# Attention values projected once in channel layout, with their taps on ScalarE and VectorE

## The chip, the cores and the metric

One core of a Trainium2 chip runs the whole program. The metric is the time of one execution on the device in microseconds. TensorE, VectorE, ScalarE, GpSimd and SyncE (the queue SP that starts DMAs) each have their own in-order instruction stream and hand work over through semaphores.

## The reference

Sixteen sequences of 750 tokens with 128 channels go through one layer: a token pooler that halves the length to 375, an attention block with 8 heads of 64, and a mixture of 16 experts with a shared path. Only the attention's projections matter here. `xn` is the normalized sequence, padded with two zeros ahead in time:

```
def _proj(xp, w1, wd):
    y = jnp.einsum('ed,bdn->ben', w1, xp)
    y = wd[None, :, 0:1] * y[..., :-2] + wd[None, :, 1:2] * y[..., 1:-1] + wd[None, :, 2:3] * y[..., 2:]
    return y
xp = jnp.pad(xn.transpose(0, 2, 1), ((0, 0), (0, 0), (2, 0)))
q = _split_heads(_proj(xp, wq1, wqd), b, n) * scale
k = _split_heads(_proj(xp, wk1, wkd), b, n)
v = _split_heads(_proj(xp, wv1, wvd), b, n)
```

Each of q, k and v has 512 channels; each channel is filtered along time by its own three taps.

## The kernel before

The program has four blocks. Block one is the pooler's network, block two does everything up to the tables of the experts for all 16 batches, block three is the shared path and a search for thresholds, and then come the lists and the experts.

Block two, which the change edits, is a software pipeline written out by hand. `bodies` runs `body(b, u)` for b from -3 to 17 on every engine, and a body has 8 steps h. A pair of steps (c = h // 2, part = h % 2) handles two heads of batch b: `scores` on TensorE (part 0 the last third of the queries, part 1 the rest), `biased_max` on VectorE, `exps` on ScalarE. One pair later come `transpose_probs` on TensorE, `copy_probs` on ScalarE, and on VectorE a reciprocal (L961) and `precw` (L963), which TensorE transposes along (L645). Two pairs later come `attend` (L659) and VectorE's `OT` (L952). Other batches' work is spread over the same steps: pooling of batch b + 2 in h = 1 (`pool_tokens`, L700), whose result VectorE copies to `Hall` (L1006); the output projection of batch b - 1 in h = 3 (L749), added by VectorE (L1030) with statistics behind it; the transposes of normalized tokens in h = 4 (L706); gate logits in h = 7 (L771). GpSimd and VectorE make `cellmax` and `overlap` (L999) for batch b + 3 in steps 2 to 7.

Q and K are made in channel layout (128 channels of two heads on the partitions, time along the row). In the even steps TensorE projects 128 channels of batch b + 1 into the PSUM banks G0 (Q) and G1 (K), three matmuls each of split fp32 (`PASSES`: high by high, high by low, low by high). ScalarE makes the first tap from PSUM (`first_tap`, L806), VectorE the second and the third (L972, L978).

V is made in token layout (125 tokens on the partitions, 512 channels along the row), since `attend` takes it as weights. Block one scales the V weights by each of the three taps (`wvtap`, twelve products on GpSimd), and in steps 3, 5 and 7 `project_v` (L688) runs nine matmuls of 512 columns into G0 for one tile of 125 tokens: three taps, each a shifted window of the tokens, by three passes. ScalarE copies the bank to `V` (L836).

At the start of block two the weights are transposed on TensorE (L777), rounded by ScalarE (L860) and split by VectorE (L944), one group of four transposes for each of Q, K and the three scaled V weights.

Of the kernel before, what the change touches and what calls it, by code (L numbers as in the profile page):

```python
# [14 lines left out]
N = T // 2  # L15
PT_ = 125
TT_, NT = T // PT_, N // PT_
D = 512
# [39 lines left out]
def build(nc, x, tW1, tb1, tW2, tb2, tW3, tb3, gamma, beta, wq1, wqd, wk1, wkd, wv1, wvd, wout,  # L58
          gate_w, ew1, eb1, ew2, eb2, sw1, sb1, sw2, sb2, out):
    ctx = ExitStack()  # L60
    with ctx:
# [41 lines left out]
        WQKT = sbm("WQKT", [128, 2, 2, D], F32R)  # L103
        WVT = sbm("WVT", [128, 2, 3, D], F32R)
        WOT = sbm("WOT", [128, DC, 128])
# [20 lines left out]

        at = [0, DC * D, DC * D + 3 * D, DC * D + 6 * D, DC * D + 7 * D]
        W2 = tTall[:, at[0]:at[1]].rearrange("p (k n) -> p k n", n=D)
        wraw = tTall[:, at[1]:at[2]].rearrange("p (n m d) -> p n m d", n=3, m=DC)
        wvtap = tTall[:, at[2]:at[3]].rearrange("p (n m d) -> p n m d", n=3, m=DC)  # L130
        woraw = tTall[:, at[3]:at[4]]

# [3 lines left out]
        with ExitStack() as one:  # L136
# [99 lines left out]
            def _(pool):  # L236
# [25 lines left out]
                nc.gpsimd.tensor_scalar(qkd[:, 0], qkd[:, 0], -(DH ** -0.5), None, ALU.mult).then_inc(s_prep, 1)  # L262
                for a in range(3):
                    for m in range(DC):
                        nc.gpsimd.tensor_scalar(wvtap[:, a, m], wraw[:, 2, m], vd[:, m, a:a + 1], None,
                                                ALU.mult).then_inc(s_prep, 1)

# [198 lines left out]
        with ExitStack() as two:  # L466
# [30 lines left out]
            xzero = sb_("xzero", [128, 2, 2, 2])  # L497
            tap0 = sb_("tap0", [128, 2, N])
            tap1 = sb_("tap1", [128, 2, N])
            QK = sb_("QK", [128, 2, DC, N])  # L500
# [34 lines left out]
            s_qk = sem("s_qk_ready")  # L535
            s_vp = sem("s_v_in_psum")
            s_v = sem("s_v_ready")
            s_sp = sem("s_scores_in_psum")
# [30 lines left out]
            split_weights = [(wraw[:, n], WQKT[:, :, n]) for n in range(2)]  # L569
            split_weights += [(wvtap[:, a], WVT[:, :, a]) for a in range(3)]  # L570

# [36 lines left out]
            def pair_before(b, c, back):  # L608

                return b + (c - back) // 4, (c - back) % 4  # L610

            PARTS = ((2,), (1, 0))
# [3 lines left out]
            def _(pe):  # L616
# [33 lines left out]
                def attend(b, c, u):  # L650
                    n, r = 4 * b + c, c % 2
                    pe.wait_ge(s_pt0, 2 * n + 2)
                    pe.wait_ge(s_pt1, 2 * n + 2)
                    pe.wait_ge(s_v, 3 * b + 3)
                    wait(pe, s_o, n)
                    for j in range(NT):
                        half, at, w = min(j, 1), (j // 2) * 2 * PT_, N - j * PT_
                        for q in range(2):
                            last = nc.tensor.matmul(bO[DH * q:DH * (q + 1), j * PT_:N],  # L659
                                                    V[:, u, j, (2 * c + q) * DH:(2 * c + q + 1) * DH],  # L660
                                                    PT[:PT_, r, 2 * q + half, at:at + w],
                                                    start=(j == 0), stop=(j == NT - 1))
                    last.then_inc(s_pv, 1)

                def project_qk(m, c, u):
                    pe.wait_ge(s_xt, m + 1)
                    for n, g in enumerate((G0, G1)):
                        if n == 0 and c > 0:

                            wait(pe, s_v, 3 * m + c)  # L670
                        elif n == 0:
                            wait(pe, s_qk, 8 * m - 1)
                        else:
                            wait(pe, s_qk, 8 * m + 2 * c)
                            if c == 0:
                                wait(pe, s_pc, m - 2)
                            if c == 3:
                                wait(pe, s_lm, 2 * (m - 1))
                        for n_, (a, x_) in enumerate(PASSES):
                            last = nc.tensor.matmul(g[:, :XE], WQKT[:, a, n, c * 128:(c + 1) * 128], xnThl[:, u, x_],  # L680
                                                    start=(n_ == 0), stop=(n_ == 2))
                        last.then_inc(s_qkp, 1)

                def project_v(m, t, u):
                    pe.wait_ge(s_qk, 8 * m + 2 * t + 1)
                    for a in range(3):
                        for n_, (x_, w_) in enumerate(PASSES):
                            last = nc.tensor.matmul(G0[:PT_, :], xnThl[:, u, x_, t * PT_ + a:(t + 1) * PT_ + a],  # L688
                                                    WVT[:, w_, a], start=(a == 0 and n_ == 0),
                                                    stop=(a == 2 and n_ == 2))  # L690
                    last.then_inc(s_vp, 1)

                def pool_tokens(m, u):
# [15 lines left out]
                def body(b, u):  # L709
                    v_ = 1 - u  # L710
                    for h in range(HEADS):
# [11 lines left out]
                        if p in (2, 4, 6) and valid(b + 1):  # L723
                            project_qk(b + 1, p // 2 - 1, v_)
                        m, d = pair_before(b, c, 1)
                        if valid(m):
# [6 lines left out]
                        if h == 1 and valid(b - 2):  # L733
                            m = b - 2

                            pe.wait_ge(s_qk, cap(8 * b + 8, 8 * B))
                            pe.wait_ge(s_lf, 3 * m + 3)
# [4 lines left out]
                        if h == 3 and valid(b - 1):  # L742
# [9 lines left out]
                            last.then_inc(s_wo, 1)  # L752
                        if p in (3, 5, 7) and valid(b + 1):
                            project_v(b + 1, (p - 3) // 2, v_)
                        if h == 4 and valid(b + 2):
# [9 lines left out]
                        if h == 7 and valid(b - 1):  # L765
                            m = b - 1
                            pe.wait_ge(s_tt, m + 1)
                            pe.wait_ge(s_qk, cap(8 * (b + 1) + 6, 8 * B))
                            wait(pe, s_pc, cap(m, B))
# [12 lines left out]
            def _(act):  # L782
# [26 lines left out]
                def body(b, u):  # L809
                    for h in range(HEADS):  # L810
# [3 lines left out]
                        if p in (0, 2, 4, 6) and valid(m):  # L814
                            first_tap(m, d, 0)
                            first_tap(m, d, 1)
                        m, d = pair_before(b, c, 1)
                        if part == 1 and valid(m):
# [7 lines left out]
                        if h not in (1, 2) and valid(m):  # L826
# [3 lines left out]
                            nc.scalar.activation(Wt[:, k], overlap[:, k % 2], ACT.Relu).then_inc(s_wt, 1)  # L830
                        if p in (3, 5, 7) and valid(b + 1):
                            m, t = b + 1, (p - 3) // 2
                            act.wait_ge(s_vp, 3 * m + t + 1)

                            wait(act, s_pv, 4 * (m - 1))
                            nc.scalar.copy(V[:, 1 - u, t], G0[:PT_, :]).then_inc(s_v, 1)  # L836
                        if h == 4 and valid(b + 2):
# [78 lines left out]
            def _(dve):  # L916
# [21 lines left out]
                def body(b, u):  # L938
                    for h in range(HEADS):
# [15 lines left out]
                        if valid(b):  # L955
                            biased_max(b, c, part)
                        m, d = pair_before(b, c, 1)
                        if part == 0 and valid(m):
# [694 lines left out]
```

## Time and profile before

| | before |
|---|---|
| median of 3 runs | 1475.83 us (1474.38 to 1475.99) |
| profiled execution | 1474.93 us, span 1473.2 us |
| TensorE busy over the span | 1267.5 us, 86% |
| VectorE busy | 775.3 us, 53% |
| ScalarE busy | 696.9 us, 47% |
| GpSimd busy | 411.4 us, 28% |
| block two, first and last TensorE group | 409 to 1117 us |

The span runs from the first to the last instruction of the profiled execution. The durations of matmuls overlap, since they are pipelined: the distance between two starts says more than a duration. PE is TensorE, PEld its weight loads, DVE VectorE, ACT ScalarE, POOL GpSimd. The shares are means over blocks with different limits, so block two is read by itself.

### The profile page before, as it was taken

What the parts mean: (1) busy time and instruction counts of PE and PEld (TensorE: products, weight loads), DVE (VectorE), ACT (ScalarE), POOL (GpSimd) and SP (SyncE); (2) the same over time, 40 slices, a digit from 0 to 9 for tenths busy, and PEclk for the clock granted to TensorE, in tenths of its full rate; (3) what the DMA queues carried; (4) which work ended last, traced back from release to release, by engine and by line L of the source; (5) the groups of instructions that cost most, each with busy time, mean ns of one, the idle gap of its engine ahead of it and who ended that gap; (6) DMA issues with size and microseconds to landing.
All of it is one profiled execution on the core that took longest, in us unless ns stands there. A gap on an engine that the chain in (4) does not pass through costs nothing. (4 is left out here: it accounts for less than half of the span.)

```text
span 1473.2 us, 24382 instructions
## 1 busy us (share of the span) xinstructions
PE 1267.5 (86%) x8097; PEld 1039.9 (71%) x8097; DVE 775.3 (53%) x2387; ACT 696.9 (47%) x1759; POOL 411.4 (28%) x391
## 2 busy tenths in 40 slices
PE   6999999999658999999999999999985993656663
PEld 5999999999556677777777777777754883445552
DVE  4343333443455767777776776776643667311121
ACT  2333333433334777776676777776752340021111
POOL 7000000000044223333333232331005001388885
PEclk9999999999868999999999999999997996787777
DMA  4000000000010000000000000000000111055442
GB/s 113 11 23 20 12 21 11 22 17 15 16 32 22 1 23 23 18 19 13 23 23 23 23 24 23 23 7 13 13 20 23 32 36 48 19 97 85 84 84 39
DMA packets 93857, 44.06 MB, mean 30 GB/s; under 512 B 31295, under 2 KB 90088, under 8 KB 93752
## 3 DMA queue, kind: packets, MB, share of 16 engines
q1 hardware_dynamic: 69960, 36.25, 9.3%
q0 software_dynamic: 23808, 6.69, 3.5%
q8 instruction: 48, 0.79, 0.2%
q14 instruction: 41, 0.34, 0.1%
HBM read 29.52 MB, written 10.18 MB: 27 GB/s over the span
## 5 line engine op out<-in xcount | busy, mean ns | idle before, releaser
L287 PE MATMUL bank<-h1hl,W2hl 128*128 128x376 f32 x1536 | 277.2, 336 | 2.7 <-DVE h1hl L402 2.7
L287 PEld LDWEIGHTS bank<-h1hl,W2hl 128*128 128x128 f32 x1536 | 263.2, 189 | 3.1 <-DVE h1hl L402 3.1
L788 ACT ACTIVATE P<-P,nmax 125x375 f32<-125x375 f32 (+2 forms) x384 | 188.6, 499 | 3.7 <-DVE nmax L933 3.6
L933 DVE CUSTOM_DVE_ANT_0 P<-bank,nbias 125x375 f32<-125x375 f32 (+2 forms) x384 | 139.3, 411 | 66.0 <-PE bank L626 65.7
L364 ACT ACTIVATE h<-bank,b2c 128x375 f32<-128x375 f32 x128 | 73.6, 575 | 205.4 <-PE bank L287 205.4
L798 ACT COPY PT<-bank 128x500 f32<-128x500 f32 (+1 forms) x256 | 127.2, 548 | 57.0 <-PE bank L645 37.2
L901 POOL TENSOR_SCALAR cellmax<-grid,csb 125x375 f32<-125x375 f32 x96 | 121.1, 1271 | 43.0 <-DVE overlap L999 42.6
L1579 ACT ACTIVATE hE<-bank,EB 128x375 f32<-128x375 f32 x64 | 36.8, 574 | 198.7 <-PE bank L1554 196.1
L626 PE MATMUL bank<-QK 64*125 64x375 f32 (+2 forms) x768 | 115.5, 405 | 2.8 <-DVE nmax L933 2.8
L806 ACT ACTIVATE tap<-bank,qkd 128x375 f32<-128x375 f32 x128 | 71.1, 575 | 97.6 <-PE bank L680 97.3
L639 PE MATMUL bank<-ident,P 125*128 125x125 f32 x768 | 113.8, 275 | 3.9 <-ACT P L788 3.9
L688 PE MATMUL bank<-WVT,xnThl 128*125 128x512 f32 x432 | 113.6, 408 | 2.5 <-DVE QK L978 2.5
L870 POOL MEMSET xzero<- 128x8 f32 x1 | 0.1, 106 | 378.4 <-POOLq L136 378.4
L680 PEld LDWEIGHTS bank<-xnThl,WQKT 128*128 128x128 f32 x384 | 63.6, 191 | 57.3 <-issue 57.3
L1517 POOL DMA_INDIRECT out_dram<-yE,ids x48 | 95.6, 1991 | 27.5 <-issue 23.1
L680 PE MATMUL bank<-xnThl,WQKT 128*128 128x378 f32 x384 | 86.5, 355 | 19.2 <-ACT V L836 10.7
L639 PEld LDWEIGHTS bank<-ident,P 125*128 125x128 f32 x768 | 87.6, 141 | 15.6 <-ACT P L788 5.2
L659 PE MATMUL bank<-PT,V 125*64 125x375 f32 (+2 forms) x768 | 96.5, 386 | 0.5 <-issue 0.5
L688 PEld LDWEIGHTS bank<-WVT,xnThl 128*125 128x125 f32 x432 | 77.7, 189 | 19.0 <-DVE QK L978 3.1
L877 POOL TENSOR_SCALAR lnve<-lnmv 125x3 f32<-125x3 f32 x16 | 3.2, 198 | 306.5 <-DVE lnmv L923 306.5
L626 PEld LDWEIGHTS bank<-QK 64*125 64x125 f32 x768 | 62.4, 182 | 31.9 <-issue 26.0
L276 PEld LDWEIGHTS bank<-xThl,W1hl 128*128 128x128 f32 x396 | 68.2, 192 | 22.6 <-issue 21.9
(195 smaller groups left out, 2236.3 us busy)
## 6 DMA issues: line engine op xcount, KB each, us to landing
X<-in_x_dram SPq DMA_DIRECT2D x34, 375.0 KB
EW<-in_L_ffn_w_dram SPq DMA_DIRECT2D x32, 256.0 KB
token_table<-row SPq DMA_DIRECT2D x16, 210.9 KB
tTall<-tT SPq DMA_DIRECT2D x16, 187.5 KB, 2.4
out_dram<-oS SPq DMA_DIRECT2D x16, 187.5 KB
tTall<-in_L_tok_W_dram SPq DMA_DIRECT2D x1, 1024.0 KB, 7.0
EB<-in_L_ffn_b_dram SPq DMA_DIRECT2D x16, 62.5 KB
tok<-token_table,ids POOLq DMA_INDIRECT x48
```

The lines of the kernel that those rows point to most:

```text
L287: last = nc.tensor.matmul(bank[4 + m % 2][:, :NE], W2hl[:, a, k, m * 128:(m + 1) * 128], h1hl[:, p, b, k], start=(k == 0 and n == 0), stop ...
L364: nc.scalar.activation(h2[:, p, m], bank[4 + m % 2][:, :N], ACT.Gelu, bias=b2c[:, m:m + 1]).then_inc(s_g2, 1)
L626: last = nc.tensor.matmul(bS[q][:PT_, at:at + w], QK[r:r + DH, 0, c, i * PT_:(i + 1) * PT_], QK[r:r + DH, 1, c, :w], start=True, stop=True)
L639: last = nc.tensor.transpose(bT[half][:, k * PT_:(k + 1) * PT_], P[:, 2 * r + q, f:f + 128], ident[:PT_, :PT_])
L659: last = nc.tensor.matmul(bO[DH * q:DH * (q + 1), j * PT_:N], V[:, u, j, (2 * c + q) * DH:(2 * c + q + 1) * DH], PT[:PT_, r, 2 * q + half, ...
L680: last = nc.tensor.matmul(g[:, :XE], WQKT[:, a, n, c * 128:(c + 1) * 128], xnThl[:, u, x_], start=(n_ == 0), stop=(n_ == 2))
L688: last = nc.tensor.matmul(G0[:PT_, :], xnThl[:, u, x_, t * PT_ + a:(t + 1) * PT_ + a], WVT[:, w_, a], start=(a == 0 and n_ == 0), stop=(a ...
L788: nc.scalar.activation(P[:, 2 * r + q, SEG[i]:SEG[i] + w], P[:, 2 * r + q, SEG[i]:SEG[i] + w], ACT.Exp, bias=nmax[:, 2 * r + q, i:i + 1], ...
L798: nc.scalar.copy(PT[:, r, 2 * q + half, 0:w], bT[half][:, :w]).then_inc((s_pt0, s_pt1)[half], 1)
L901: nc.gpsimd.tensor_scalar(cellmax[:, k % 2], grid0[:], csb[:, TT_ + k:TT_ + k + 1], None, ALU.max).then_inc(s_cm, 1)
L933: nc.vector.tensor_tensor_reduce(out=P[:, 2 * r + q, SEG[i]:SEG[i] + w], in0=bS[q][:PT_, at:at + w], in1=nbias[:, 2 * c + q, (2 - i) * PT_ ...
L1517: nc.gpsimd.indirect_dma_start(out=out_rows, out_offset=bass.IndirectOffsetOnAxis(ap=ids[r][k][:, 0:1], axis=0), in_=yE[:, r % 2, k], in_o ...
```

## The change

V is projected like Q and K, once, in channel layout: 128 channels at a time, three matmuls of 378 columns into G0 (`project_v`, now four groups a batch). ScalarE makes the first tap into `tap0[:, 2]`, VectorE the second and the third into `VT`. TensorE transposes the three blocks of 125 tokens of `VT` into G1 (`transpose_v`), and ScalarE copies them to `V`. Chunks 0, 1 and 2 of batch b + 1 are projected in steps 3, 5 and 7 of body b, chunk 3 of batch b in step 1; each is transposed two steps later. Both stand between `scores` and `transpose_probs` in TensorE's order; on ScalarE the V copy and the V tap stand ahead of `copy_probs` and `exps` of the step; on VectorE the V taps follow `biased_max`. The scaled weights, their twelve GpSimd products, and two of three V weight groups at the start of block two are gone. The waits on the banks G0 and G1 follow the new order.

```diff
-        WVT = sbm("WVT", [128, 2, 3, D], F32R)
+        WVT = sbm("WVT", [128, 2, D], F32R)
...
-                for a in range(3):
-                    for m in range(DC):
-                        nc.gpsimd.tensor_scalar(wvtap[:, a, m], wraw[:, 2, m], vd[:, m, a:a + 1], None,
-                                                ALU.mult).then_inc(s_prep, 1)
...
-            split_weights += [(wvtap[:, a], WVT[:, :, a]) for a in range(3)]
+            split_weights += [(wraw[:, 2], WVT)]
...
+            def value_step(b, h):
+
+                p = projection_step(b, h)
+                return (b, 3) if p == 1 else (b + 1, (p - 3) // 2) if p < HEADS else (-1, 0)
...
-                    pe.wait_ge(s_v, 3 * b + 3)
+                    pe.wait_ge(s_v, n + 1)
...
-                        if n == 0 and c > 0:
-
-                            wait(pe, s_v, 3 * m + c)
-                        elif n == 0:
-                            wait(pe, s_qk, 8 * m - 1)
+                        if n == 0:
+
+                            wait(pe, s_vt, 4 * m + c)
                         else:
-                            wait(pe, s_qk, 8 * m + 2 * c)
+
+                            wait(pe, s_v, 4 * m + c - 1)
...
-                def project_v(m, t, u):
-                    pe.wait_ge(s_qk, 8 * m + 2 * t + 1)
-                    for a in range(3):
-                        for n_, (x_, w_) in enumerate(PASSES):
-                            last = nc.tensor.matmul(G0[:PT_, :], xnThl[:, u, x_, t * PT_ + a:(t + 1) * PT_ + a],
-                                                    WVT[:, w_, a], start=(a == 0 and n_ == 0),
-                                                    stop=(a == 2 and n_ == 2))
+                def project_v(m, c, u):
+                    pe.wait_ge(s_qk, 8 * m + 2 * c + 1)
+                    for n_, (a, x_) in enumerate(PASSES):
+                        last = nc.tensor.matmul(G0[:, :XE], WVT[:, a, c * 128:(c + 1) * 128], xnThl[:, u, x_],
+                                                start=(n_ == 0), stop=(n_ == 2))
                     last.then_inc(s_vp, 1)
+
+                def transpose_v(m, c):
+                    pe.wait_ge(s_vt, 4 * m + c + 1)
+
+                    pe.wait_ge(s_qk, min(8 * m + 2 * c + 4, 8 * B))
+                    for t in range(NT):
+                        last = nc.tensor.transpose(G1[:PT_, t * 128:(t + 1) * 128], VT[:, t * PT_:(t + 1) * PT_],
+                                                   ident[:])
+                    last.then_inc(s_vtp, 1)
...
+                        m, d = value_step(b, h)
+                        if part == 1:
+                            n, e = (m, d - 1) if d else (m - 1, 3)
+                            if valid(n):
+                                transpose_v(n, e)
+                            if valid(m):
+                                project_v(m, d, m % 2)
...
-                        if p in (3, 5, 7) and valid(b + 1):
-                            project_v(b + 1, (p - 3) // 2, v_)
...
+                        if part == 1:
+                            m, d = value_step(b, h)
+                            n, e = (m, d - 1) if d else (m - 1, 3)
+                            if valid(n):
+                                act.wait_ge(s_vtp, 4 * n + e + 1)
+
+                                wait(act, s_pv, 4 * (n - 2) + e + 1)
+                                nc.scalar.copy(V[:, n % 2, :, e * 128:(e + 1) * 128],
+                                               G1[:PT_, :NT * 128].rearrange("p (t d) -> p t d", d=128)
+                                               ).then_inc(s_v, 1)
+                            if valid(m):
+                                act.wait_ge(s_vp, 4 * m + d + 1)
+
+                                wait(act, s_vt1, 4 * m + d)
+                                nc.scalar.activation(tap0[:, 2], G0[:, 0:N], ACT.Copy,
+                                                     scale=vd[:, d, 0:1]).then_inc(s_vt0, 1)
...
-                            nc.scalar.copy(V[:, 1 - u, t], G0[:PT_, :]).then_inc(s_v, 1)
...
+                        m, d = value_step(b, h)
+                        if part == 1 and valid(m):
+                            n = 4 * m + d
+                            dve.wait_ge(s_vt0, n + 1)
+                            nc.vector.scalar_tensor_tensor(out=tap1[:, 2], in0=G0[:, 1:N + 1], scalar=vd[:, d, 1:2],
+                                                           in1=tap0[:, 2], op0=ALU.mult, op1=ALU.add
+                                                           ).then_inc(s_vt1, 1)
+                            dve.wait_ge(s_vt1, n + 1)
+
+                            wait(dve, s_vtp, n)
+                            nc.vector.scalar_tensor_tensor(out=VT[:], in0=G0[:, 2:N + 2], scalar=vd[:, d, 2:3],
+                                                           in1=tap1[:, 2], op0=ALU.mult, op1=ALU.add
+                                                           ).then_inc(s_vt, 1)
```

## Rows read from the trace of the kernel before

**Rows 1.** Windows, one period: length, busy us and count by engine, clock, DMA share, GB/s.

```profile
749.91:790.75 40.84, 39.68 (x285) 30.46 (x283) 29.58 (x105) 29.27 (x86) 12.95 (x14) 1.00 0.07 21
```

**Rows 2.** Waits in the same period: total us, times, longest.

```profile
DVE P L933 <- PE bank L626: 3.9, 3, 1.8
...
DVE Hall L1006 <- PE bank L700: 3.2, 1, 3.2
...
DVE lmax L1038 <- PE bank L771: 1.9, 1, 1.9
...
DVE Hall L1030 <- PE bank L749: 1.4, 1, 1.4
...
PE bank L645 <- DVE precw L963: 0.4, 1, 0.4
```

**Rows 3.** Timeline of TensorE: start us, duration us, instructions, idle before.

```profile
444.58 2.33 PE L688 MATMUL bank<-WVT,xnThl 128*125 128x512 f32 x9
447.67 1.28 PE L680 MATMUL bank<-xnThl,WQKT 128*128 128x378 f32 x6 [0.77 <-ACT V L836]
...
749.91 4.10 PE L700 MATMUL bank<-X,Wt 125*125 125x128 f32 x36
753.85 0.48 PE L739 MATMUL bank<-ident,row 125*16 125x125 f32 x3
...
761.29 2.79 PE L749 MATMUL bank<-WOT,OT 128*125 128x128 f32 x24
763.83 2.34 PE L688 MATMUL bank<-WVT,xnThl 128*125 128x512 f32 x9
...
769.09 1.49 PE L659 MATMUL bank<-PT,V 125*64 125x375 f32 x12
...
770.98 0.91 PE L626 MATMUL bank<-QK 64*125 64x250 f32 x8
771.82 0.54 PE L639 MATMUL bank<-ident,P 125*128 125x125 f32 x3
...
772.65 2.34 PE L688 MATMUL bank<-WVT,xnThl 128*125 128x512 f32 x9
774.91 0.90 PE L626 MATMUL bank<-QK 64*125 64x375 f32 x4
776.37 1.28 PE L680 MATMUL bank<-xnThl,WQKT 128*128 128x378 f32 x6 [0.55 <-ACT V L836]
777.49 0.81 PE L639 MATMUL bank<-ident,P 125*128 125x125 f32 x6
778.13 0.27 PE L645 MATMUL bank<-ident,precw 125*128 125x125 f32 x1
...
790.75 4.10 PE L700 MATMUL bank<-X,Wt 125*125 125x128 f32 x36
...
1036.46 0.90 PE L626 MATMUL bank<-QK 64*125 64x375 f32 x4 [0.57 <-DVE nmax L933]
...
1072.16 0.90 PE L626 MATMUL bank<-QK 64*125 64x375 f32 x4 [0.61 <-DVE nmax L933]
```

**Rows 4.** Timeline of VectorE in steps 4 and 5 of a period.

```profile
767.16 0.55 DVE L933 CUSTOM_DVE_ANT_0 P<-bank,nbias 125x375 f32<-125x375 f32 x1 [1.55 <-PE bank L626]
...
768.70 0.60 DVE L972 SCALAR_TENSOR_TENSOR tap<-bank,qkd,tap 128x375 f32<-128x375 f32 x1
769.33 0.61 DVE L978 SCALAR_TENSOR_TENSOR QK<-bank,qkd,tap 128x375 f32<-128x375 f32 x1
769.86 0.60 DVE L972 SCALAR_TENSOR_TENSOR tap<-bank,qkd,tap 128x375 f32<-128x375 f32 x1
...
773.60 0.54 DVE L1014 TENSOR_TENSOR xnThl<-xnT,xnThl 128x375 fp32r<-128x375 f32 x1
```

**Rows 5.** Timeline of ScalarE at the end of step 5.

```profile
775.25 0.51 ACT L830 ACTIVATE Wt<-overlap 125x375 f32<-125x375 f32 x1
775.65 0.57 ACT L836 COPY V<-bank 125x512 f32<-125x512 f32 x1
```

More of the change, by code:

```diff
@@ L123, in build @@
         PASSES = ((0, 0), (0, 1), (1, 0))
-        at = [0, DC * D, DC * D + 3 * D, DC * D + 6 * D, DC * D + 7 * D]
+        at = [0, DC * D, DC * D + 3 * D, DC * D + 4 * D]
         W2 = tTall[:, at[0]:at[1]].rearrange("p (k n) -> p k n", n=D)
         wraw = tTall[:, at[1]:at[2]].rearrange("p (n m d) -> p n m d", n=3, m=DC)
-        wvtap = tTall[:, at[2]:at[3]].rearrange("p (n m d) -> p n m d", n=3, m=DC)
-        woraw = tTall[:, at[3]:at[4]]
+        woraw = tTall[:, at[2]:at[3]]
         out_rows = out.rearrange("b n c -> (b n) c")
@@ L497, in build @@
             xzero = sb_("xzero", [128, 2, 2, 2])
-            tap0 = sb_("tap0", [128, 2, N])
-            tap1 = sb_("tap1", [128, 2, N])
+            tap0 = sb_("tap0", [128, 3, N])
+            tap1 = sb_("tap1", [128, 3, N])
+            VT = sb_("VT", [128, N])
             QK = sb_("QK", [128, 2, DC, N])
@@ L536, in build @@
             s_vp = sem("s_v_in_psum")
+            s_vt0 = sem("s_v_tap0_ready")
+            s_vt1 = sem("s_v_tap1_ready")
+            s_vt = sem("s_vT_ready")
+            s_vtp = sem("s_vT_transposed_in_psum")
             s_v = sem("s_v_ready")
@@ L734, in body @@
                             m = b - 2
-                            pe.wait_ge(s_qk, cap(8 * b + 8, 8 * B))
+                            pe.wait_ge(s_v, min(4 * b + 3, 4 * B))
                             pe.wait_ge(s_lf, 3 * m + 3)
@@ L767, in body @@
                             pe.wait_ge(s_tt, m + 1)
-                            pe.wait_ge(s_qk, cap(8 * (b + 1) + 6, 8 * B))
+                            pe.wait_ge(s_v, min(4 * (b + 1) + 2, 4 * B))
                             wait(pe, s_pc, cap(m, B))
@@ L830, in body @@
                             nc.scalar.activation(Wt[:, k], overlap[:, k % 2], ACT.Relu).then_inc(s_wt, 1)
[L831 to L835, printed above, removed]
-                            nc.scalar.copy(V[:, 1 - u, t], G0[:PT_, :]).then_inc(s_v, 1)
                         if h == 4 and valid(b + 2):
```

## The prediction

> **What bounds the kernel now.** I read the page first (busy tenths, granted clock), then the windows of attention block two, the waits inside one of its periods, and the timelines of TensorE, VectorE and ScalarE there. The change touches nothing outside block two (405 to 1122 us), but for twelve GpSimd products in block one.
>
> Block two repeats itself. The 36 matmuls of `pool_tokens` start at 749.91 and again at 790.75 [rows 3]: 40.84 us for a batch. In it TensorE is busy 39.68 us, its weight loads 30.46, VectorE 29.58 and ScalarE 29.27, all at the full granted clock [rows 1]. VectorE's idle time is nearly all waiting for TensorE: 3.9 us for scores, 3.2 for pooled tokens, 1.9 for gate logits, 1.4 for the output projection [rows 2]. TensorE waits in turn 0.6 us for ScalarE's V copy [rows 3] and 0.4 for `precw` [rows 2]. So TensorE sets the pace, by issue time rather than by an idle partner, and two engines at 72% follow closely.
>
> **The change part by part.** TensorE's durations overlap, so I price by distances between starts. Nine V matmuls of 512 columns: 772.65 to 774.91, 2.26 us [rows 3]; three groups a batch, and the one ahead of the short gate matmuls is 0.1 shorter, so 6.7 us go. Added: 12 matmuls of 378 columns in four groups; six such take 776.37 to 777.49, 0.187 each [rows 3], so 2.25 us. Added: 12 transposes; six take 777.49 to 778.13, 0.107 each [rows 3], so 1.3 us (their identity has 128 columns for 125). TensorE's own work falls by 6.7 - 2.25 - 1.3 = 3.15 us a batch.
>
> The Trainium skill (TensorE: Matmul & The Clock Gate, Part 4: PE-mode transpose) gives about 275 ns to a transpose in a kernel's context and adds the copy out of PSUM. By it the twelve would cost 3.3 us and the saving would be 1.1. The trace has that number as a duration, but starts lie 0.107 apart; the trace decides.
>
> VectorE gets 8 SCALAR_TENSOR_TENSOR a batch, of the form of the taps it has: tap to its dependent 0.63 us, that to the next 0.53 [rows 4]; 4 x 1.16 = 4.6 us. 29.6 + 4.6 = 34.2 us. ScalarE gets four taps and four copies for three copies. The nearest rows: a copy or tap lasts 0.57, of which the last 0.1 overlap the next instruction (at 775.65 a copy starts before the 0.51 of the one at 775.25 are over [rows 5]); four taps and one more copy, less the three copies' greater width (my estimate 0.1 each): 5 x 0.5 - 0.3 is 2.2 at least, 5 x 0.57 is 2.85 at most; I take 2.4, to 31.7 us. TensorE's steps without any wait then sum to 35.8 us.
>
> Three engines at 35.8, 34.2 and 31.7 hand work to each other in strict order, so the sum isn't the answer; the steps must be walked. The costs in TensorE's order: scores 0.84 (770.98 to 771.82), Q and K projections 1.12, six transposes 0.64, attend and token transposes 1.89 (769.09 to 770.98), odd-step transposes 0.83, `pool_tokens` 3.94 (749.91 to 753.85), output projection 2.54 [rows 3]. A step h=4 or 5 of VectorE: biased maxima, reciprocal and `precw` 1.54 (767.16 to 768.70), four taps 2.3; from 767.16 to the end of the last one at 774.14 the two steps take 7.0 us, to be 8.1 with the V taps [rows 4]. TensorE's two steps without waits become 4.7 + 2.6 = 7.3. So steps 4 to 7 (no large TensorE group in them) turn VectorE-bound, while steps 1 and 3, with pooling and output projection, leave VectorE free to catch up. Two waits carry that over: `precw`, which the transposes need and which comes 1.5 us after VectorE begins the step, and ScalarE's exps, which end late (775.25 [rows 5]) and later by the V copy and tap now queued before `copy_probs` and the exps.
>
> The walk, from the start of `pool_tokens`, old starts of TensorE's steps from the trace (h3, h4, h5, h6, h7, h0, h1, next pooling): 9.6, 16.2, 21.1, 25.0, 30.3, 34.8, 39.1, 40.84. New:
> - h3 9.6. Scores, V transposes, V projection, probabilities' transposes, output projection: 0.84 + 0.33 + 0.56 + 0.87 + 2.54, so h4 at 14.8. VectorE's V taps fall in its old wait for the output projection: nothing.
> - h4: residual and statistics keep VectorE until 16.5, 0.7 after the scores are there; `precw` is late by 0.8. h5 at 20.3.
> - h5: no large group; h6 at 22.9. VectorE is done with V tap 2 at 24.1: the Q projection waits 0.45 for it; the exps hold the transposes 0.2, `precw` 0.5. h7 at 28.8.
> - h7: h0 at 32.0. Late logits shift (K's bank) and `precw`: 0.4. h1 at 36.65. K's tap done 0.05 late. Pooling at 39.33.
>
> Saving a batch: 40.84 - 39.33 = 1.5 us, half of TensorE's 3.15; the rest becomes waits for VectorE. The same walk with the old order, with these rules, gives the old starts within 0.1 us.
>
> Twelve periods run between the first full and the last full batch: 12 x 1.5 = 18.1. The last batches have no tokens to pool and no `overlap` (0.6 us x 6), so VectorE is freer: batch 14 goes from 1036.46 to 1072.16 [rows 3], 35.7 us, against 31.4 of TensorE work, and I give batches 13 and 14 2.4 and 2.2. Batch 0 has no output projection to hide VectorE's taps behind: 0.5. Batch 15 gets a V projection and 6 transposes it did not have: +1.0. At the start of block two V matmuls at 444.58 and the 0.77 us wait for their copy stand between pooling and the next projection [rows 3]: 3.1 us that move ahead of pooling as 0.6 and are partly replaced by a wait for V's and K's taps; 1.5 of gain, between 0 and 3. Weight transposes, 24 to 16, their three casts and splits to one, and GpSimd's twelve products: nothing; the former lie behind pooling, the products behind the whole of block one. If that cover went, two casts and two splits would be about 2 us. Nothing is added to SP's or GpSimd's queues. Sum: 18.1 + 2.4 + 2.2 + 0.5 + 1.5 - 1.0 = 23.7 us.
>
> The profiled execution took 1474.93 us with a span of 1473.2, 0.9 under the median of 1475.83; the saving is taken from the median: 1452.
>
> **Rivals.**
> - All of TensorE's saving arrives (VectorE's added taps find its 10.4 us of waits [rows 2]): 3.15 x 15 is 47 us, 1429. Against: 5 of those 10.4 us lie at pooling and output projection and can't move.
> - VectorE takes over entirely and its old waits stay: per batch +4.6 for taps, -3.15 where its waits for TensorE shrink: +1.5, or 22 us, 1498. Place: steps h4 to h7, through `precw` and the Q projection's wait for V's second tap. It decides from the point where under 3.15 of the 4.6 us falls into waits. For: VectorE is the later one in most steps of my walk. Against: the taps of steps 1 and 3, half of the 4.6, fall in waits that stay.
>  The Trainium skill (Perfetto Trace Analysis, section Identifying the Most-Contended Engine) calls matmul busy time a poor measure and wants weight-load busy time instead; by it TensorE stands at 75%, close to VectorE's 72, and VectorE would be the bound after. The trace's V groups are solid without waits, so TensorE is the bound before.
> - The transposes cost TensorE their duration, 0.275: saving 1.1 less what waits eat, about 0.5 a batch: 8 us, 1468. Against: [rows 3].
> - Given back: waits eat all. An extra 0.2 us at each of eight hand-overs is 1.5 a batch, and the time stays 1475.
>
> **Chances.** Forecast 0.65: 0.3 to 2.6 us a batch instead of 1.5, which are 14 us later or 13 earlier over twelve batches, so 1438 to 1468 with the ramp's bounds inside. All of it 0.09; transposes dear 0.05; given back 0.08; VectorE over 0.13. The range 1436 to 1477 leaves out most of the first rival and of the last, some 0.19. No change means within 0.2%, 3 us, about what this kernel's three runs (1474.38 to 1475.99) can tell. Faster 0.79, same 0.08, slower 0.13.
>
> **What the profile after would show.** A period of 39.3 us between starts of `pool_tokens`; TensorE's busy sum down some 3 us and idle time of it up, in waits of the transposes for `precw` (L645) and exps (L639) and of the Q projection for V's second tap; VectorE 34 us a period with its waits for scores mostly gone, those for pooling and output projection kept; starts of V projections 0.19 apart, V transposes 0.11. I am wrong if VectorE's waits at pooling vanish (then it is the bound over the whole period), if the new taps last over 0.63 us, or if the exps, pushed back by ScalarE's two new instructions, hold the transposes in every step.

## The result and the profile after

The changed kernel takes 1457.8 us against 1475.6 in the same comparison (medians of four executions each), a ratio of 0.987 with an interval of 0.986 to 0.989: faster by 1.3%. The forecast was 1452 within 1436 to 1477, so the direction and the range held, and the gain was 18 us where 24 were forecast. One of the four executions of the changed kernel ran slow (1534 us, mean clock 0.80 for 0.92); slow executions are left out of every ratio here, and without it the median is 1457.6.

The period of block two, answering to [rows 1]: length, busy microseconds and counts of TensorE, its weight loads, VectorE, ScalarE and GpSimd, then clock, DMA share and GB/s.

```profile
744.93:784.24 39.31, 37.81 (x282) 29.10 (x281) 33.73 (x113) 31.30 (x91) 12.93 (x14) 1.00 0.08 22
```

39.31 us for a batch instead of 40.84, where the walk had given 39.33. VectorE went from 29.58 to 33.73 (34.2 forecast), ScalarE from 29.27 to 31.30 (31.7 forecast). The waits in that period, answering to [rows 2] (total us, times, longest):

```profile
DVE Hall L1045 <- PE bank L711: 2.8, 1, 2.8
...
DVE Hall L1069 <- PE bank L767: 1.1, 1, 1.1
DVE tap L987 <- ACT tap L847: 0.8, 2, 0.4
PE bank L650 <- DVE precw L1002: 0.7, 2, 0.4
PE bank L684 <- DVE VT L993: 0.4, 1, 0.4
```

VectorE's waits for scores and gate logits are gone; those for pooling and output projection are still there. TensorE waits for V's second tap and for `precw`. Its busy sum fell by 1.9 us (39.68 to 37.81), where some 3 were forecast, and the time in the period that the sum leaves rose only from 1.2 to 1.5. Its timeline, answering to [rows 3], with the first group of every step from 3 on and more of steps 4 to 6:

```profile
744.93 4.09 PE L711 MATMUL bank<-X,Wt 125*125 125x128 f32 x36
...
754.56 0.91 PE L631 MATMUL bank<-QK 64*125 64x250 f32 x8
...
759.92 0.90 PE L631 MATMUL bank<-QK 64*125 64x375 f32 x4
760.75 1.31 PE L684 MATMUL bank<-xnThl,WQKT 128*128 128x378 f32 x6
761.90 0.81 PE L644 MATMUL bank<-ident,P 125*128 125x125 f32 x6
763.02 0.33 PE L650 MATMUL bank<-ident,precw 125*128 125x125 f32 x1 [0.32 <-DVE precw L1002]
...
765.17 0.91 PE L631 MATMUL bank<-QK 64*125 64x250 f32 x8
766.00 0.59 PE L700 MATMUL bank<-ident,VT 128*125 128x128 f32 x3
766.35 0.76 PE L691 MATMUL bank<-xnThl,WVT 128*128 128x378 f32 x3
766.95 0.48 PE L644 MATMUL bank<-ident,P 125*128 125x125 f32 x3
...
767.90 0.90 PE L631 MATMUL bank<-QK 64*125 64x375 f32 x4
769.16 1.28 PE L684 MATMUL bank<-xnThl,WQKT 128*128 128x378 f32 x6 [0.36 <-DVE VT L993]
...
773.62 0.91 PE L631 MATMUL bank<-QK 64*125 64x250 f32 x8
...
776.92 0.90 PE L631 MATMUL bank<-QK 64*125 64x375 f32 x4
...
781.51 0.91 PE L631 MATMUL bank<-QK 64*125 64x250 f32 x8
...
784.24 4.09 PE L711 MATMUL bank<-X,Wt 125*125 125x128 f32 x36
```

A V group costs 0.35 for three transposes (I had 0.33) and 0.60 for three matmuls (I had 0.56), 0.95 together for 0.89. The difference over four groups is 0.24, so TensorE was relieved by 6.7 - 3.8 = 2.9 us a batch rather than by 3.15.

By starts, the 2.9 - 1.5 = 1.4 us that don't arrive lie mostly in three steps: step 4 is 0.4 us longer than before, step 6 also 0.4, although its wait of 0.55 for the V copy is gone, and step 0 is 0.3 longer. These are the waits for V's second tap, for the exps and for `precw`.

Where the time went, by starts of the same groups. The twelve full periods, from the pooling in batch 1 to that in batch 13, took 490.2 us before and 471.1 after, 19.0 less (18.1 forecast). From there to block three's first group it is 127.4 and 123.9, 3.5 less (3.6 forecast). Between the pooling in batch 0 and in batch 1 it is 39.0 and 37.9, 1.1 less (0.5). The start of block two, though, was to be 1.5 us shorter and is longer. The first listing is of the kernel before, the second of the changed one. Each begins with the matmuls on the cumulative sums that end block one and ends with the pooling in batch 0.

```profile
405.96 2.67 PE L343 MATMUL bank<-ident,cs 16*125 16x16 f32 x12 [14.05 <-DVE cs L455]
...
465.86 5.86 PE L700 MATMUL bank<-X,Wt 125*125 125x128 f32 x36 [2.00 <-ACT Wt L830]
```

```profile
407.07 2.67 PE L338 MATMUL bank<-ident,cs 16*125 16x16 f32 x12 [14.01 <-DVE cs L450]
...
451.39 0.56 PE L700 MATMUL bank<-ident,VT 128*125 128x128 f32 x3 [3.00 <-DVE QK L1017]
451.70 1.02 PE L691 MATMUL bank<-xnThl,WVT 128*128 128x378 f32 x3
455.29 2.23 PE L684 MATMUL bank<-xnThl,WQKT 128*128 128x378 f32 x6 [2.57 <-DVE VT L993]
...
471.87 6.08 PE L711 MATMUL bank<-X,Wt 125*125 125x128 f32 x36
```

59.9 us before, 64.8 after: 4.9 more, of which 1.5 are there at the pooling in batch -1 (32.8 and 34.3 us behind the first row). Block one itself ended 1.1 later in this execution; that isn't the change's, since the runs below that keep the old block one have this row between 406.5 and 407.0. Windows of the stretch 440 to 480, first of the kernel before, then of the changed one, give the granted clock in the third number from the right:

```profile
440.00:480.00 40.00, 32.25 (x172) 26.09 (x173) 22.10 (x67) 18.45 (x45) 17.23 (x17) 0.88 0.07 20
```

```profile
440.00:480.00 40.00, 28.69 (x138) 24.73 (x139) 22.51 (x61) 15.80 (x36) 10.91 (x12) 0.68 0.04 12
```

TensorE waited 3.0 and 2.6 us there, where the kernel before waits 1.4 for K's tap and 0.8 for the V copy; from the pooling in batch -1 to that in batch 0 its waits sum to 11.1 us for 6.8. It ran at a mean clock of 0.68 for 0.88, so for much of the stretch at the lower of its two levels, 1.2 GHz.

### The profile page after: what moved, and what is told of

Its sections match the earlier page's. It is cut to its first block and busy times, and to the rows that moved or that the text cites. A ratio compares the mean times of both kernels' runs of the same rounds, so it can differ in the third digit from the quotient of the medians.

```text
span 1455.9 us, 24666 instructions
## 1 busy us (share of the span) xinstructions
PE 1241.1 (85%) x8041; PEld 1022.9 (70%) x8041; DVE 842.4 (58%) x2513; ACT 727.7 (50%) x1837; POOL 401.9 (28%) x379
## 5 line engine op out<-in xcount | busy, mean ns | idle before, releaser
L684 PE MATMUL bank<-xnThl,WQKT 128*128 128x378 f32 x384 | 91.2, 365 | 17.4 <-DVE VT L993 9.1
L684 PEld LDWEIGHTS bank<-xnThl,WQKT 128*128 128x128 f32 x384 | 64.8, 195 | 58.3 <-issue 58.3
L644 PEld LDWEIGHTS bank<-ident,P 125*128 125x128 f32 x768 | 90.9, 141 | 16.3 <-ACT P L804 12.2
L421 DVE COPY zsb<-bank 128x375 f32<-128x375 f32 x32 | 17.6, 549 | 119.3 <-PE bank L292 119.3
L350 ACT ACTIVATE h<-bank,b1c 128x376 f32<-128x376 f32 x132 | 70.1, 576 | 28.5 <-PE bank L271 28.5
L271 PE MATMUL bank<-xThl,W1hl 128*128 128x376 f32 x396 | 78.9, 348 | 2.9 <-DVE xThl L387 2.7
L1017 DVE SCALAR_TENSOR_TENSOR QK<-bank,qkd,tap 128x375 f32<-128x375 f32 x128 | 77.9, 608 | 4.5
## 6 DMA issues: line engine op xcount, KB each, us to landing
EB<-in_L_ffn_b_dram SPq DMA_DIRECT2D x16, 62.5 KB
```

What stands on the lines that cost most here:

```text
L271: last = nc.tensor.matmul(bank[L1_BANKS[m]][:, :NE], W1hl[:, a, m * 128:(m + 1) * 128], xThl[:, p, b], start=(n == 0), stop=(n == 2))
L644: last = nc.tensor.transpose(bT[half][:, k * PT_:(k + 1) * PT_], P[:, 2 * r + q, f:f + 128], ident[:PT_, :PT_])
L1017: nc.vector.scalar_tensor_tensor(out=QK[:, q, d], in0=ps[:, 2:N + 2], scalar=qkd[:, q, d, 2:3], in1=tap1[:, q], op0=ALU.mult, op1=ALU.add) ...
```

## The experiments

All times are medians; ratios are against the kernel before, run on the same chip beside them. The unit for the middle of block two is the period between pooling starts: 40.84 before, 39.31 after. The blocks behind block two, which no edit touches, last 349.3 to 352.2 us in the profiled executions, so differences of a microsecond or two in the total prove little by themselves.

**VectorE's added taps left out.** The second and third tap of V aren't computed, and the three blocks are transposed from the first tap.

```diff
                             wait(pe, s_v, 4 * m + c - 1)
+                            wait(pe, s_qk, 8 * m + 2 * c)
...
-                                wait(act, s_vt1, 4 * m + d)
-                                nc.scalar.activation(tap0[:, 2], G0[:, 0:N], ACT.Copy,
-                                                     scale=vd[:, d, 0:1]).then_inc(s_vt0, 1)
+                                wait(act, s_vtp, 4 * m + d)
+                                nc.scalar.activation(VT[:], G0[:, 0:N], ACT.Copy,
+                                                     scale=vd[:, d, 0:1]).then_inc(s_vt, 1)
```

> The changed kernel without VectorE's two V taps (ScalarE's first tap goes straight into VT; the second and third tap of V are left out, and the K projection waits for K's taps directly). VectorE loses 4.6 us a batch. Theory A, hand-overs: the walk with these rules gives 38.1 us a period for 39.3, so some 18 us less than the changed kernel's 1457.8: 1440. Theory B, VectorE alone is the bound after the change: 4.6 x 15 is 69 us less, 1389. Theory C, TensorE is still the bound: no difference, 1458.

1443.0 us, ratio 0.978 (0.976 to 0.981): 15 us less than the change. But its period is only 0.33 shorter, 38.98:

```profile
734.44 4.10 PE L712 MATMUL bank<-X,Wt 125*125 125x128 f32 x36
...
760.01 0.86 PE L644 MATMUL bank<-ident,P 125*128 125x125 f32 x6 [0.45 <-ACT P L805]
...
771.65 0.56 PE L701 MATMUL bank<-ident,VT 128*125 128x128 f32 x3 [0.32 <-DVE QK L1005]
...
773.42 4.10 PE L712 MATMUL bank<-X,Wt 125*125 125x128 f32 x36
```

4.6 us less on VectorE bring 0.33. Where TensorE had waited for `VT` it now waits 0.45 for the exps, and 0.32 for K's tap; its waits for `precw` are still 0.7 us. Theories B and C are out, and A's size is wrong too (38.1 forecast): the exps, which the walk put behind, stand just behind the taps. That the time is near the walk's 1440 is luck: the twelve full periods give only 4 of the 15 us. The pooling in batch 0 comes 59.1 us after block one's last group for 64.8, so 5.7 are at the start of block two, where the V taps were on the path, 2.4 more come before the pooling in batch 1, and 2.1 after that in batch 13.

**One matmul for three in each V projection.** The two matmuls with a low part are left out.

```diff
-                    for n_, (a, x_) in enumerate(PASSES):
-                        last = nc.tensor.matmul(G0[:, :XE], WVT[:, a, c * 128:(c + 1) * 128], xnThl[:, u, x_],
-                                                start=(n_ == 0), stop=(n_ == 2))
+                    last = nc.tensor.matmul(G0[:, :XE], WVT[:, 0, c * 128:(c + 1) * 128], xnThl[:, u, 0],
+                                            start=True, stop=True)
```

> The changed kernel with one matmul in each V projection for three (the two low-part passes of V are left out). TensorE loses 8 x 0.19 = 1.5 us a batch. Theory A, hand-overs: only steps 1 and 3, where TensorE is alone with its large groups, give it back: 0.75 a batch, 1447. Theory B, VectorE the bound: 1458. Theory C, TensorE the bound: 1436.

1438.2 us, ratio 0.975 (0.973 to 0.976), period 38.33: 0.98 of the 1.5 us arrive in a period, between A (0.75) and C (1.5). By these two runs TensorE's work is worth about nine times as much as that of VectorE's V taps: 0.65 us a period per microsecond against 0.07. The time itself is nearer to C's 1436 than to A's 1447, since the start of block two, the stretch from batch 0 to 1 and the end of the block each give 1.6 us besides the twelve periods.

**TensorE's relief alone, in the kernel before.** Five of nine matmuls in a V group: parts of the second tap and all of the third are left out.

```diff
+                    some = [(a, p) for a in range(3) for p in PASSES][:5]
+                    for n_, (a, (x_, w_)) in enumerate(some):
+                        last = nc.tensor.matmul(G0[:PT_, :], xnThl[:, u, x_, t * PT_ + a:(t + 1) * PT_ + a],
+                                                WVT[:, w_, a], start=(n_ == 0), stop=(n_ == 4))
```

> The kernel before with five of its nine matmuls in each V group (parts of the second and all of the third tap are left out): TensorE's relief alone, 12 x 0.25 = 3.0 us a batch, close to the 3.15 of the change, with nothing new on VectorE and ScalarE. Theory A, the half that the change lost went to the added V taps and their hand-overs: 2.3 to 2.8 of the 3.0 arrive, period near 38.3, time near 1436. Rival: the coupling of the engines would have eaten half of any relief, with or without taps: 1.5 a batch, 1453.

1460.8 us, ratio 0.990 (0.988 to 0.992), period 39.89: only 0.95 of the 3.0 arrive. The rival's side, and less than it gave. A period, and then the wait in it that names the place (total, times, longest):

```profile
746.27 4.09 PE L699 MATMUL bank<-X,Wt 125*125 125x128 f32 x36
...
786.16 4.09 PE L699 MATMUL bank<-X,Wt 125*125 125x128 f32 x36
```

```profile
PE bank L680 <- ACT V L835: 2.4, 2, 1.5
```

TensorE finishes V earlier and then waits for ScalarE's V copy before it may project Q into the same bank: 2.4 us a batch for 0.6 in the kernel before. The copy is queued behind `copy_probs`, the exps and the relu. So a relief of the kind forecast isn't passed on where V stood; something else in the change must have opened this.

**VectorE's load alone, in the kernel before.** Two spare instructions in each odd step.

```diff
+                        if part == 1 and valid(b):
+                            for k in range(2):
+                                nc.vector.scalar_tensor_tensor(out=spare[:PT_, k], in0=grid0[:],
+                                                               scalar=mhalf[:, 0:1], in1=grid1[:],
+                                                               op0=ALU.mult, op1=ALU.add)
```

> The kernel before with two more SCALAR_TENSOR_TENSOR of 125 x 375 behind the biased maxima of each odd step, 8 a batch (about 4.3 us on VectorE), that wait for nobody and that nobody waits for: VectorE's load alone. Theory A: they fit into waits that the old order has; 0 to 0.3 us a batch, 1476 to 1480. Theory B, VectorE's load counts in full: 4.3 x 15, 1540.

1476.9 us, ratio 1.0007 (0.9997 to 1.0016), period 40.84. VectorE's busy time rose to 33.74 in the window of the period, as much as in the changed kernel, and cost nothing:

```profile
751.90:792.74 40.84, 39.70 (x285) 30.46 (x283) 33.74 (x113) 29.26 (x86) 12.96 (x14) 1.00 0.07 21
```

**The places of the change, in the kernel before.** All nine matmuls stay. `project_v` is moved from behind `attend` and the other batches' work to the place between `scores` and `transpose_probs`, and ScalarE's V copy ahead of `copy_probs`.

```diff
                             project_qk(b + 1, p // 2 - 1, v_)
+                        if p in (3, 5, 7) and valid(b + 1):
+                            project_v(b + 1, (p - 3) // 2, v_)
...
                             first_tap(m, d, 1)
+                        if p in (3, 5, 7) and valid(b + 1):
+                            m, t = b + 1, (p - 3) // 2
+                            act.wait_ge(s_vp, 3 * m + t + 1)
+
+                            wait(act, s_pv, 4 * (m - 1))
+                            nc.scalar.copy(V[:, 1 - u, t], G0[:PT_, :]).then_inc(s_v, 1)
```

> The kernel before with the places of the change alone: the nine matmuls of a V group between scores and the probabilities' transposes, and ScalarE's V copy ahead of copy_probs and the exps. Computes the same, with the same work. Theory G, the place is what lets a relief of TensorE arrive: by itself it does little or harms, since the 0.6 us wait for the V copy goes and copy_probs and the exps come 2.3 us later in the step: period 40.8 to 41.5, 1475 to 1487. Rival: the early V copy alone is worth the wait that it removes, 40.3, 1468.

1482.5 us, ratio 1.0044 (1.0031 to 1.0058). The period is 41.45:

```profile
753.10 4.10 PE L700 MATMUL bank<-X,Wt 125*125 125x128 f32 x36
...
794.55 4.10 PE L700 MATMUL bank<-X,Wt 125*125 125x128 f32 x36
```

The places by themselves cost 0.6 us a batch, inside theory G's bounds; the rival's 1468 is out.

**The places and the relief together.** The same moves and five of nine matmuls.

> The same places, and five matmuls of nine in a V group (parts of the second and all of the third tap are left out): 3.0 us a batch off TensorE. Without the new places this relief gave a period of 39.90 for 40.84, TensorE waiting 2.4 us a batch for the V copy behind the exps. Theory G: with them about 2 us arrive, period 38.8 to 39.3, 1445 to 1453. Rival: the exps set it either way, 39.9, 1461.

1441.8 us, ratio 0.977 (0.975 to 0.978), period 38.75:

```profile
733.73 4.10 PE L699 MATMUL bank<-X,Wt 125*125 125x128 f32 x36
...
772.48 4.10 PE L699 MATMUL bank<-X,Wt 125*125 125x128 f32 x36
```

With the new places 41.45 - 38.75 = 2.7 of 3.0 us arrive (the period shown is the longest of this run; but for the first, at 37.85, the others take 38.64 to 38.71); without them 0.95. Theory G holds, and more arrives than it said. The group on TensorE and the copy on ScalarE were moved together, so which of the two moves does it isn't shown; the wait for the copy in the run above speaks for the copy.

**The start of block two.** Eighteen filler matmuls into a bank that isn't in use yet.

```diff
+                        for _ in range({(-1, 3): 6, (-1, 4): 5, (-1, 5): 3, (0, 1): 4}.get((b, h), 0)):
+                            nc.tensor.matmul(bank[4][:], WQKT[:, 0, 0, 0:128], WQKT[:, 0, 0], start=True, stop=True)
```

> The changed kernel with 18 filler matmuls of 512 columns into a bank that nobody reads yet, put ahead of TensorE's four long waits at the start of block two (batch -1 steps 3, 4, 5: six, five, three; batch 0 step 1: four). Computes the same. Theory D: the start of block two became 4.9 us longer because TensorE idles in the new waits and its granted clock falls to 0.5; filled, the clock stays up and half of the 4.9 or more comes back: 1453 to 1455 beside 1457.8. Rival E: the waits for V's and K's taps are the cause and the clock hangs on nothing: 1458 or, where fillers stand ahead of real work, up to 1462.

1453.0 us, ratio 0.984 (0.983 to 0.986), 4.8 under the change. The clock from 440 to 480 is 0.92 for 0.68, and the pooling in batch 0 comes 62.5 us after the end of block one (406.03 to 468.55) for 64.8:

```profile
440.00:480.00 40.00, 28.95 (x174) 24.62 (x174) 25.04 (x66) 18.56 (x43) 15.33 (x16) 0.92 0.07 20
```

To the pooling in batch 1 it is 99.3 us for 102.7. But 0.6 of these 3.4 us lie ahead of the first filler, which stands behind the pooling in batch -1. From there to the pooling in batch 1 it is 65.6 for 68.4, so 2.8 us are what the fillers gave, seen in starts; the rest of the medians' 4.8 isn't located, and the profiled executions differ by only 2.2 (1455.5 and 1457.6). Up to the pooling in batch 0 the fillers gave 1.7 of the 3.4 us by which the way from batch -1 had grown. What is left is put down to the waits for V's and K's taps themselves: the run without V's taps, which has no fillers, is 5.3 us shorter than the changed kernel there, and its clock from 440 to 480 is 0.82 for 0.68.

**Loads moved to GpSimd.** First the `overlap` as two GpSimd instructions instead of one on VectorE:

```diff
+                            nc.gpsimd.tensor_scalar(cellmin[:], grid1[:], csb[:, k:k + 1], None,
+                                                    ALU.min).then_inc(s_cn, 1)
+                            pool.wait_ge(s_cn, 6 * m + k + 1)
+                            nc.gpsimd.tensor_tensor(overlap[:, k % 2], cellmin[:], cellmax[:, k % 2],
+                                                    ALU.subtract).then_inc(s_ov, 1)
```

> The changed kernel with the overlap of the pooling weights made on GpSimd (a minimum and a subtraction) for VectorE's one instruction: VectorE loses 6 x 0.53 = 3.2 us a batch, GpSimd gets about 6 x 2.1 = 12.5. Computes the same. Theory A: like leaving out part of the V taps; 0.7 to 1.0 us a batch less, 1443 to 1448. Rival F: GpSimd's chain (cellmax, the new pair, normalization steps behind them in its queue) ends later than today's and holds the transposes of tokens and the pooling weights, or slows VectorE's copies: 1458 to 1480.

1480.5 us, ratio 1.003 (1.0019 to 1.004). The period did fall, to 39.1, but the first pooling of block two now waits for GpSimd's longer chain:

```profile
433.03 6.61 PE L713 MATMUL bank<-X,Wt 125*125 125x128 f32 x36 [18.96 <-ACT Wt L864]
```

against 419.39 in the changed kernel; the pooling in batch 0 is at 501.05 for 471.87. VectorE lost its six `overlap` instructions, but its busy time fell by 2.4 us (33.73 to 31.33) for the 3.2 expected. That bought 0.2 a period, and the chain at the start cost 29. This is rival F. Then the relu of the pooling weights on GpSimd instead of ScalarE:

```diff
-                            nc.scalar.activation(Wt[:, k], overlap[:, k % 2], ACT.Relu).then_inc(s_wt, 1)
+                            nc.gpsimd.tensor_scalar(Wt[:, k], overlap[:, k % 2], 0.0, None, ALU.max).then_inc(s_wt, 1)
```

> The changed kernel with the relu of the pooling weights on GpSimd for ScalarE: ScalarE loses 6 x 0.42 = 2.5 us a batch, GpSimd gets about 6 x 1.25 = 7.5. Computes the same. Tells how much of the remaining waits are ScalarE's: if the exps' end holds TensorE's transposes in steps 6 and 0, 0.3 to 0.6 us a batch come back, 1449 to 1453; if VectorE's precw is the later one, nothing: 1458.

1468.3 us, ratio 0.994 (0.993 to 0.996); period 39.58, and 10 us more at the start. In the period TensorE's waits for `precw` rose from 0.7 to 1.2 us, and VectorE's `precw` copy takes 531 ns on the mean for 445. So it doesn't tell what ScalarE's queue is worth, since it slowed VectorE.

**Statistics behind the taps.** On VectorE the normalization statistics of steps 1 and 3 move into steps 2 and 4, behind the taps and the overlap, for all but the first and last batches; GpSimd takes its normalization steps in 3 and 5.

```diff
+                        if h == 2 and b >= 0 and valid(b + 2):
+                            m, base = b + 2, LN * (b + 2)
+                            wait_apart(dve, s_lnd, base + 1, s_on[0])
+                            ln_stats(lambda t: Hall[:, m, t], lnstat, lnmv, s_lnd, base + 1)
+                        if h == 4 and b <= 14 and valid(b - 1):
+                            m, base = b - 1, LN * (b - 1)
+                            wait_apart(dve, s_g, base + 1, s_on[0])
+                            ln_stats(lambda t: Hall[:, m, t], gstat, gmv, s_g, base + 1)
```

> The changed kernel with VectorE's normalization statistics (0.8 us each, twice a batch) moved from ahead of the biased maxima of steps 2 and 4 to behind the taps of these steps, and GpSimd's steps that need them one or two steps later. Computes the same. Theory H: what is left of TensorE's 3.15 us is lost where precw comes late behind residual, copy and statistics: 0.35 at each of steps 2 and 4 and what their rows hide; 0.6 to 1.2 us a batch come back, 1441 to 1449 for 1457.8. Rival: the exps hold the transposes next, 0 to 0.3 us a batch, 1453 to 1458.

1448.2 us, ratio 0.981 (0.980 to 0.982), 9.6 under the change. Three periods take 116.70 (741.94 to 858.64), 38.90 each, 0.4 less: short of H's 0.6 to 1.2. That the time is inside H's bounds is luck in part: of the 9.4 us between the two profiled executions the twelve periods give 4.4 and the end of the block 2.0, while 1.8 lie in the blocks behind, which the edit doesn't touch. The `precw` waits of steps 2 and 4 shrink, but one of 0.88 appears in step 6, behind the moved work:

```profile
768.19 0.33 PE L650 MATMUL bank<-ident,precw 125*128 125x125 f32 x1 [0.88 <-DVE precw L1008]
```

> Late statistics together with the filler matmuls at the start of block two, which took 4.7 us off the changed kernel by themselves. Computes the same. If the two are independent the gains add: 4 to 5 us under the late statistics alone. Theory H: 1437 to 1445.

1447.0 us, ratio 0.980 (0.979 to 0.981), the fastest that computes everything as before; but only 1.2 under the run without fillers, whose interval it meets, where 4 to 5 were expected. By starts the fillers do give 2.3 us (65.8 for 68.1 from the pooling in batch -1 to that in batch 1). The profiled execution loses them again far behind the fillers: 1.1 us after the pooling in batch 13 and 2.9 in the blocks behind block two. Why is not known; with the fillers alone, 1.1 and 1.0 us were lost in these places.

## Why the prediction was right, and where it was wrong

- **TensorE sets the pace before: right.** VectorE's load alone is free there (1.0007), a cut in TensorE's isn't, though only 0.95 of 3.0 us of it arrive.
- **Removed and added work: right, 0.24 us short.** Three matmuls of the form of the Q and K rows take 0.60 where six take 1.12, so I was 0.04 short in each group; transposes with an identity of 128 columns cost 0.117 each for 0.107, another 0.02. The rival with 0.275 a transpose is out by the starts.
- **The walk of the period: right in its sum, 39.33 for 39.31, and in each step's start within 0.2 us.** Its reading was wrong in part, so the sum owes something to luck. I put the half of TensorE's relief that is lost down to VectorE's added taps in steps 4 to 7. Leaving them out gives 0.33 us. TensorE's waits for `precw` come to 0.7 us a period in the changed kernel, and also in the run without V's taps and in the kernel before with the new places, so the added taps aren't what makes `precw` late. The experiments split the period like this: the new places +0.6, TensorE's relief of 2.9 at the rate of the run with both (2.7 of 3.0) -2.6, the taps on VectorE +0.3, together 39.1. The 0.2 to 39.31 are what is left for ScalarE's V tap and extra copy; that share is a remainder and was not tried by itself, and that the parts may be added, though they were measured in different kernels, is assumed.
- **A cause that I did not name:** the change makes TensorE's freed time usable by moving the V group and its copy ahead of the exps. I had counted the 0.55 us wait for the copy as a wait that goes, not as the wall that any relief runs into.
- **VectorE takes over: wrong for the middle.** Its slope was 0.07 us a microsecond, by the run without taps. The condition of that rival, less than 3.15 of 4.6 us in waits, wasn't near: all but 0.33 of the 4.6 cost nothing, in part because the exps come just behind the taps.
- **The start of block two: wrong, the step that cost the forecast its 6 us.** The sentence gave "1.5 of gain, between 0 and 3"; it was a loss of 4.9. I priced the removed V matmuls and allowed for "a wait for V's and K's taps" without walking it: each V projection is now followed by copy, tap, tap before the next Q projection, with nothing else to do in batches -1 and 0. Waits of 3.0 and 2.6 us resulted, for 1.4 and 0.8 before, and TensorE's clock fell with them. The V projection that moved ahead of the pooling in batch -1 took 1.1 us there, at the lower clock, for the 0.6 that I gave. The fillers show the clock's part, some 2.8 us to the pooling in batch 1; that the rest is the waits' is argued from what is left over.
- **The end of block two: right** (3.5 for 3.6). Batch 0 gave twice what I had (1.1 for 0.5).

## What to carry to other kernels

Before a relief of the pacing engine is priced, look for the wait that it will run into: here the bank's next use waited for a copy queued behind other work on ScalarE, and 3.0 us less of matmuls were worth 0.95 or 2.7, depending on where the group and its copy stood. A walk of one period can have the right sum while the wrong edit gets the blame; leave each part out once. And walk the ramp as carefully as the steady part: long matmul groups that look like waste there may be part of what keeps the clock up (0.88 with nine matmuls in a V group, 0.77 with five in the same places).

## What the runs showed of the hardware

TensorE's clock was the unexpected part. The stretch from 440 to 480 us had a mean granted clock of 0.88 in the kernel before, 0.68 in the changed one, with shorter V groups and longer gaps, 0.82 in it without V's second and third tap, and 0.92 with fillers; the 36 pooling matmuls in batch 0 lasted 5.86, 6.08 and 4.91 us in the kernel before, the changed one and the one with fillers, and 4.10 at full clock. The Trainium skill (TensorE: Matmul & The Clock Gate, the table under Why this matters for your kernels) advises against idle gaps of TensorE between bursts of matmuls, since they bring the lower rate back; the trace of the changed kernel agrees: behind its gaps of 3.0 and 2.6 us the mean granted clock was 0.50 from 455 to 465 us.
